# Four-layer sequence kernel on one Trainium2 core: every eighth product dt*u*B of the scans moves from VectorE to GpSimd, from a copy of B that ScalarE takes out of PSUM

## What is computed

```python
x_dbl = einsum('bsd,ed->bse', u, x_proj_w)
dt_r, B, C = split(x_dbl, [64, 80], axis=-1)
dt = softplus(einsum('bsr,dr->bsd', dt_r, dt_proj_w) + dt_proj_b)   # 512 channels
A = -exp(A_log)                                                     # 512 x 16
def step(h, (dt_t, B_t, C_t, u_t)):
    h = h * exp(dt_t[:, :, None] * A) + (dt_t * u_t)[:, :, None] * B_t[:, None, :]
    y = einsum('bdn,bn->bd', h, C_t)
```

## Time and profile before

| what | us |
| --- | --- |
| median of three runs | 2286.82 (2285.85 to 2292.27) |
| the profiled execution | 2285.53 |
| its span | 2283.7 |
| the scans in it | 89 to 1612 |
| busy: TensorE | 1945.9 (85%) |
| busy: VectorE | 1862.5 (82%) |
| busy: ScalarE | 1194.6 (52%) |
| busy: GpSimd | 1150.0 (50%) |

### The profile page before, as it was taken

One profiled execution on the slowest core, in us unless ns is written; L12 is line 12 of the kernel. 1 busy time (PEld: TensorE's weight loads), 2 busy tenths in 40 slices (PEclk: granted clock), 3 DMA queues, 4 the chain that ended last, 5 costly groups with the idle time before them and its releaser, 6 DMA issues.

```text
span 2283.7 us, 19266 instructions
## 1 busy us (share of the span) xinstructions
PE 1945.9 (85%) x6016; PEld 775.7 (34%) x6016; DVE 1862.5 (82%) x2189; ACT 1194.6 (52%) x2143; POOL 1150.0 (50%) x584
## 2 busy tenths in 40 slices
PE   6688998979899888878788888889788879999986
PEld 2223333324243233333232323234554323333323
DVE  2667989889899999889898999898766488888823
ACT  2535455445556565544555556454352246666673
POOL 2466767768878877668687777665200000000000
PEclk8799999989999999989999999999997779999998
DMA  5142122122222222222222222222014052230001
GB/s 184 39 136 61 62 65 69 53 70 68 72 65 73 72 75 70 62 65 73 63 70 70 74 71 76 68 88 83 24 61 52 8 107 30 37 43 9 2 2 37
DMA packets 80714, 143.20 MB, mean 63 GB/s; under 512 B 14587, under 2 KB 19643, under 8 KB 80076
## 3 DMA queue, kind: packets, MB, share of 16 engines
q1 hardware_dynamic: 80612, 141.98, 23.0%
HBM read 132.34 MB, written 9.01 MB: 62 GB/s over the span
## 4 chain that ended last, share of the span: by engine, by line
PE 51%; DVE 24%; POOL 11%; issue 6%; ACT 5%; DMA 1%; SPq 1%; POOLq 0%; DVEq 0%; ACTq 0%
PE psum L1562 14%; DVE hbuf L2123 12%; POOL hbuf L1312 7%; PE psum L680 5%; PE psum L1399 5%; DVE hbuf L2108 4%; PE psum L666 4%; DVE gain L956 4%; PE psum L646 4%; PE psum L561 3%; PE psum L1542 2%; PE psum L1375 2%; PE psum L1555 2%; PE psum L1423 2%; PE psum L550 2%
## 5 line engine op out<-in xcount | busy, mean ns | idle before, releaser
L1312 POOL TENSOR_TENSOR hbuf<-hbuf,cbuf 128x1024 f32<-128x1024 f32 x384 | 903.0, 2355 | 411.7 <-ACT hlast L1923 199.9
L1562 PE MATMUL psum<-hbuf,ident 128*128 128x512 f32 x1536 | 792.5, 640 | 128.2 <-POOL hbuf L1312 127.9
L1915 ACT ACTIVATE psum<-slots,cols 128x512 f32<-128x512 f32 x768 | 524.0, 686 | 461.3 <-DVE hbuf L2123 458.3
L2108 DVE TENSOR_TENSOR hbuf<-slots,psum 128x1024 f32<-128x1024 f32 x384 | 460.2, 1199 | 94.8 <-PE psum L1542 46.8
L2123 DVE TENSOR_TENSOR_SCAN hbuf<-psum,hlast,hbuf 128x512 f32<-128x512 f32 x384 | 470.3, 1265 | 17.6 <-ACT psum L1915 17.6
L2123 DVE TENSOR_TENSOR_SCAN hbuf<-psum,hbuf 128x512 f32<-128x512 f32 x384 | 447.3, 1205 | 19.0 <-ACT psum L1915 18.8
L1562 PEld LDWEIGHTS psum<-hbuf,ident 128*128 128x128 f32 x1536 | 273.3, 196 | 449.5 <-issue 270.1
L956 DVE TENSOR_REDUCE gain<-psum 128x1 f32<-128x512 f32 x512 | 314.6, 681 | 77.9 <-PE psum L646 77.7
L646 PE MATMUL psum<-slots 99*128 99x512 bf16 x512 | 212.7, 419 | 25.8 <-DVE gain L968 13.1
L511 POOL COPY wl<-hbuf 128x512 f32<-128x512 f32 x8 | 4.8, 612 | 446.8 <-PE psum L680 418.1
L1542 PE MATMUL psum<-bcs,pick 48*128 48x512 bf16 x384 | 153.1, 399 | 63.9 <-DVE hbuf L2108 61.4
(11 more groups left out here) (261 smaller groups left out, 1938.6 us busy)
## 6 DMA issues: line engine op xcount, KB each, us to landing
cbuf<-scr_c SPq DMA_DIRECT2D x384, 256.0 KB, 3.2
slots<-scr_qk SPq DMA_DIRECT2D x96, 128.0 KB
scr_qk<-slots SPq DMA_DIRECT2D x10, 512.0 KB, 2.8
wl<-in_w SPq DMA_DIRECT2D x1, 3968.0 KB, 12.2
wl<-in_ada_w SPq DMA_DIRECT2D x1, 3584.0 KB
xt<-in_x SPq DMA_DIRECT2D x2, 1024.0 KB, 12.4
wl<-in_w SPq DMA_DIRECT2D x2, 1024.0 KB, 6.9
out<-xt SPq DMA_DIRECT2D x2, 1024.0 KB, 4.7
```

The costliest lines, as they stand in the source:

```text
L1312: pool.tensor_tensor(hs, hs, cbuf[:, at % CRING:at % CRING + 1, :].to_broadcast([P, 2, TC]), ALU.mult).then_inc(weighed, 1)
L1562: last = pe.matmul(psum[:, q, :], ident[:, :], hbuf[:, at % RING, q, :], start=False, stop=n == NS - 1, skip_group_check=True)
L1915: act.activation(decay_bank(at, q), dts[k % 2][:, e, :], ACT.Exp, scale=coefficient(WORK[k], e, n)).then_inc(decay, 1)
L2108: dve.tensor_tensor(hbuf[:, at % RING, :, :], ws[k % 2][:, 2 * p:2 * p + 2, :], psum[:, 2 + at % 2:3 + at % 2, :].to_broadcast([P, 2, TC]) ...
```

## The change

Steps with at % 8 == 4, that is h = 4, 12, 20 and 28 of each chunk, 48 in all, get their product dt*u*B from GpSimd. GpSimd issues it two steps ahead, before its product with C of step at-2. ScalarE copies the broadcast B of that step from PSUM into the new buffer `bbuf` (one, of 512 columns), also two steps ahead, at the head of its step. VectorE leaves the load out. The waits on `dbu` are counted anew, over the loads that VectorE still makes; the bank of a copied B is free for the next `spread` once the copy is done.

```diff
+def by_pool(at):
+    return at % 8 == 4
+
+def loaded_by(at, pool):
+    return sum(by_pool(n) == pool for n in range(at + 1))
...
+        bbuf = sb("bbuf", [P, TC])
...
GpSimd
+            def load(at):
+                k, h = divmod(at, HALVES)
+                p = h // NS
+                pool.wait_ge(w_ready, k * KE + 2 * p + 2)
+                pool.wait_ge(b_copied, loaded_by(at, True))
+                if at >= RING:
+                    pool.wait_ge(summed, at - RING + 1)
+                pool.tensor_tensor(hbuf[:, at % RING, :, :], ws[k % 2][:, 2 * p:2 * p + 2, :],
+                                   bbuf[:, :].rearrange("p (o t) -> p o t", o=1).to_broadcast([P, 2, TC]), ALU.mult).then_inc(dbu_pool, 1)
...
                     at = j * HALVES + h
+                    if by_pool(at + 2):
+                        load(at + 2)
                     pool.wait_ge(ld_c[at % CRING], 16 * (at // CRING + 1))
...
TensorE, spread
-                if at >= 2:
-                    pe.wait_ge(dbu, at - 1)
+                if at >= 2 and by_pool(at - 2):
+                    pe.wait_ge(b_copied, loaded_by(at - 2, True))
+                elif at >= 2:
+                    pe.wait_ge(dbu, loaded_by(at - 2, False))
...
ScalarE
+            def copy_b(at):
+                act.wait_ge(bcast, at + 1)
+                n = loaded_by(at, True)
+                if n > 1:
+                    act.wait_ge(dbu_pool, n - 1)
+                act.activation(bbuf[:, :], psum[:, 2 + at % 2, :], ACT.Identity).then_inc(b_copied, 1)
...
                     at = j * HALVES + h
+                    if by_pool(at + 2):
+                        copy_b(at + 2)
                     if at not in AHEAD:
                         decays(at, 0)
...
VectorE, scan
-                dve.wait_ge(dbu, at + 1)
+                if by_pool(at):
+                    dve.wait_ge(dbu_pool, loaded_by(at, True))
+                else:
+                    dve.wait_ge(dbu, loaded_by(at, False))
...
-                    if at + 1 < TOTAL:
+                    if at + 1 < TOTAL and not by_pool(at + 1):
                         load(at + 1)
```

More of the change, by code:

```diff
@@ L349, in build @@
         diag_ready, conv_diag_ready, out_weights_ready = sem("diag_ready"), sem("conv_diag_ready"), sem("out_weights_ready")
-        bcast, dbu, decay = sem("bcast"), sem("dbu"), sem("decay")
+        bcast, dbu, dbu_pool, decay = sem("bcast"), sem("dbu"), sem("dbu_pool"), sem("decay")
+        b_copied = sem("b_copied")
         scanned, weighed, summed = sem("scanned"), sem("weighed"), sem("summed")
@@ L1180, in convolve @@
                 if k >= 2:
-                    pool.wait_ge(dbu, HALVES * (k - 1))
+                    pool.wait_ge(dbu, loaded_by(HALVES * (k - 1) - 1, False))
                 elif k == 1:
@@ L1670, in step_in @@
                 elif k >= 2:
-                    act.wait_ge(dbu, HALVES * (k - 1))
+                    act.wait_ge(dbu, loaded_by(HALVES * (k - 1) - 1, False))
                 ps, bias = take("dt", k, e), cols[:, column:column + 1]
```

## The result

The change made the kernel slower: 2306.49 us (median of 4 runs, 2304.62 to 2307.34) against 2289.55 (4 runs, 2285.85 to 2292.93) for the kernel before on the same chip, a ratio of 1.0073 with a 95% interval of 1.0053 to 1.0094, 16.9 us. The forecast was 2300 in a range of 2285 to 2315. The profiled executions have spans of 2302.9 and 2283.7 us, 19.2 apart; that of the kernel before is one of its short ones (2285.53 us, where the median is 2289.55), hence the 2 us more.

A forecast was written before the change was run, and what follows sets the result against it. The bound was taken to change hands among VectorE, TensorE and, at chunk ends, GpSimd. Terms 10.3 + 7.1 + 1.9 + 1.6 - 7.2 = +13.7 us gave 2300 us, range 2285 to 2315.

The forecast's parts named there:

- Prices: Each added GpSimd product takes 2355 ns and each added ScalarE copy 597 ns.
- Chunk ends: From step 26, GpSimd's added product delays the next chunk: 1.49 us in even chunks, 0.27 in odd, 10.3 together.
- Chunk 2: Mainly at step 18, the waiting copy and GpSimd's added product delay the product TensorE needs: 7.1 us slower.
- Chunks 3 and 4: At step 10 the decay waits behind the copy for step 12: 1.9 and 1.6 us slower.
- Gains: Saved VectorE loads that no already full TensorE follows, in chunks 5 to 11: 7.2 us faster together.
- rival C: TensorE's clock: idle times opened on a full TensorE slow its next additions, about 2320 us; chance 0.13.
- A: VectorE sets the pace throughout the scans, so 36 saved loads give 40 us: 2257 us; chance 0.10.
- B: Earlier TensorE broadcasts halve the cost of chunks 2, 3 and 4, and three more loads count: 2292 us; chance 0.20.
- D: VectorE and GpSimd stop for each other's products, up to 111 us more: 2411 us; chance 0.02.

The follow-up runs named there:

- e3: The change, but GpSimd's products go to a spare buffer and VectorE still makes all its loads; 2324.53 us, ratio 1.0147.
- e1: The kernel before with 47 of VectorE's loads left out and nothing in their place, computation incomplete; 2274.94 us, ratio 0.993.
- e5: The change without step 28, which VectorE makes again (36 products); 2297.34 us, ratio 1.0028.
- e6: The change without step 20, which VectorE makes again (36 products); 2298.72 us, ratio 1.0033.
- e11: The change without step 12 in chunks 1 to 4 (44 products); 2302.75 us, ratio 1.0057.
- e9: The change cut to eight products: step 12 in chunks 5, 6, 9, 10 and step 4 in 6, 7, 8, 10; 2289.74 us, ratio 0.9993.
- e8: The kernel before with the last dt*u of each chunk but the first made by VectorE, nothing of the change; 2294.45 us, ratio 1.0012.
- e2: The kernel before plus ScalarE's 48 copies of B, which nothing reads; VectorE keeps all its loads; 2306.13 us, ratio 1.007.
- e4: The change with ScalarE's copy moved behind both decays and the save of its step; 2306.12 us, ratio 1.0066.
- e7: The change cut to steps 4, 12 and 20 of chunks 5, 6, 7, 9 and 10 (15 products); 2287.91 us, ratio 0.9986.
- e12: The kernel before with GpSimd's last sum of dt and dt*u both moved ahead of its product of step 29; 2247.84 us, ratio 0.9836.
- e10: The kernel before with GpSimd's last dt*u before a chunk's start moved ahead of its product of step 30; 2272.13 us, ratio 0.9917.

## Why the prediction was right

The mechanism and the place of most terms held; several sizes did not, and part of the closeness is luck. Both sides of the sum came out too small: all that was added cost 33.7 us (e3), where the sum has 20.9 and, with the small costs that it books against the gains, 25.6 (an estimate from its own terms); the loads left out saved 14.4 to 16.0 (e1), where it has 7.2, or 11.9 without those costs. The two misses cancel in part.

- **Prices.** 2359 and 598 ns, as forecast. VectorE's loads stayed at 1200 ns beside GpSimd's work.
- **Chunk ends, forecast 10.3.** Measured from scan 26 to scan 31: 1.29 to 1.46 in each even chunk (forecast 1.49), between -0.02 and 0.03 in the odd ones (forecast 0.27), together 8.6. e5 took them away. The wait at `load` rose by 2.1 us behind even chunks, as forecast. That the saved load of step 28 only lengthens this wait holds for the even chunks; behind the odd ones e1 shows it worth its full 1.1 us as long as GpSimd gets no product more; in the change nothing of it is left.
- **Chunk 2, forecast 7.1.** Measured 8.35 up to scan 26. The part from scan 16 on, forecast 6.6, was 6.2, and e6 took 6.7 away; the part before it, forecast 0.5, was 2.2. Of that 1.4 stand at scan 2, behind a start at which TensorE had half clock for 10.2 us instead of 6.8; in e5, where it is 6.8 as before and the same steps are moved up to scan 26, the chunk costs 7.1. The idle time of 11 us and the side work that comes later by 7 us show it in the rows above.
- **Chunks 3 and 4, forecast 1.9 and 1.6.** The decays came 3.5 and 4.2 late (forecast 3.0 for chunk 3) and the saved load gave back 1.1. What remained up to scan 26 was 2.9 and 3.1. In chunk 4 e11 shows that the cost is not that of step 12 alone: with it gone, lateness at scans 4, 15 and 18 takes its place.
- **Gains, forecast 7.2.** Measured 2.8, chunk ends taken out. Chunks 5, 6, 9 and 10 gave 1.2, 1.4, 1.0 and 1.6 (forecast 1.4, 1.0, 1.4, 1.0). Three places failed: chunk 7 gave 0.25 of 1.1, chunk 8 cost 0.8 where 0.55 was to be gained, chunk 11 cost 1.7 where 0.8 was to be gained. This is the term that was mis-sized. In chunks 7 and 8 no full TensorE took the gain of load 12 (it had idle times of 2.3 and 0.9 us right then): scan 13 gave it back because `nmr` was held up by GpSimd's product, by 1.3 and 1.8 us. Without these 3.0 us both chunks would have gained about what was forecast, or a little more. In e1 and e9, whose `nmr` stays at 0.14 us there, scan 13 loses nothing. The sum puts this at nothing. In chunk 11 the gain goes at scans 15 to 18, in waits for decays. And of the gains that came, the 0.8 and 1.0 at scan 3 of chunks 6 and 10 are not the saved loads': chunk 6 of e8, with no load moved, has 0.9 (rival C).

So the sum was 13.7 and the scans lost 19.5; 4.4 of the difference are gains that did not come, 1.25 chunk 2, 2.5 chunks 3 and 4, less 1.7 at the chunk ends and 0.6 in chunks 0 and 1 and ahead of them. After the scans 0.3 us were gained.

**The rivals.** A (VectorE sets the pace) fell with e1. B (the handovers hide) fell: in chunks 3 and 4 they hid next to nothing, and only in 1 and 2 was the lateness at scan 10 made good, but for 0.5 us (e11). C (TensorE's clock) is half right. It gave no dozen times 1.8 us: the clock over the scans is 0.94 against 0.95. But how long TensorE stays at half clock around a chunk's start is worth up to 3 us a chunk, up and down. The traces give for four chunks the us at half clock and how much later than before scan 3 came, counted from the chunk's first scan:

| chunk | before | change | e2 | e4 | e7 | e8 | e9 |
| --- | --- | --- | --- | --- | --- | --- | --- |
| 5 | 3.4 | 3.4, -0.2 | 6.8, +1.1 | 10.2, +2.6 | 10.2, +2.9 | 3.4, 0.0 | 10.2, +3.0 |
| 6 | 6.8 | 3.4, -0.8 | 10.2, +2.4 | 10.2, +2.3 | 3.4, -0.8 | 3.4, -0.9 | 3.4, -0.9 |
| 9 | 3.4 | 3.4, -0.3 | 6.8, +1.0 | 3.4, -0.3 | 10.2, +2.8 | 10.2, +2.7 | 10.2, +3.0 |
| 10 | 6.8 | 3.4, -1.0 | 10.2, +2.3 | 3.4, -0.9 | 3.4, -0.9 | 10.2, +1.9 | 3.4, -0.9 |

The time goes with the clock, not with the edit: e8 moves no load, and e9 none ahead of scan 3 in chunks 5 and 9. (In e12, where VectorE no longer waits at the start of chunk 9, 2.8 us were lost there with 3.4 us at half clock: something else counts, which was not traced.) That blurs each of these comparisons by about 6 us in a single execution, and two chunks at the same place (5 and 9) mostly go together. D (VectorE and GpSimd block each other) fell at its size of 111 us, since the loads and scans are free of it. But it was at work in the change itself, at VectorE's small instructions: 3.0 us at `nmr` in chunks 7 and 8. e8 shows it with a larger product. The Trainium skill (SBUF — State Buffer, Who interferes with whom) limits the lock to VectorE instructions with two SBUF inputs or in a 2-port mode, and calls it exclusive. The traces agree on both sides: load and scan, with one operand in PSUM, at 1200 ns unchanged; `nmr` and e8's product, with both inputs in SBUF, held until GpSimd's product had ended (2.2 of the 2.74 us in e8).

**Open.** Why chunk 11 lost 1.7 us was not settled: in e5 it lost nothing, in e6, which keeps its step 28, 2.0, yet the loss arises at steps 12 to 18; e9, which moves no load in chunk 11, lost 1.2 there at scan 5. The 5 us after the scans are not e4's own: the traces of e9 and e10 have 4.6 and 4.9 there, and in all three 2.7 to 2.8 of it arise 50 us behind the scans, where TensorE has half clock for 6.8 us after an idle time that the kernel before passes at full clock. The rest of it was not traced. That the spread between runs (12 to 13 us in e7, e8 and e9, 10 in the 32 runs of the kernel before) comes from the clock is likely: of those 32 the nine shortest have a mean granted clock of 0.933 to 0.935, the nine longest 0.930 or 0.931. That it comes from the chunk starts above all is argued from the traces, one for each kernel.

## What to carry to other kernels

Moving work off a busy engine is worth what that engine's idle-free stretches are worth, not its busy share: measure the ceiling by leaving the work out (here 14.4 us of 52) before you pay for the copy and the second engine. Cost what is moved by its place in the in-order queue: a 0.6 us copy that waits for a result two steps ahead holds up everything behind it, here by 3.7 us, and an operation on a half-idle engine counts in full where the next stage waits for that engine's last one. And look at that last one first: the wait of 11 times 4.2 us that stood in the profile all along was worth more when a sum and a product moved up in GpSimd's queue (37 us) than the whole moved work. When GpSimd's work moves in time, look also at VectorE's small instructions with both inputs in SBUF that it may now meet.

## What the runs showed of the hardware that was not expected

- A VectorE product of 512 columns with both inputs in SBUF lasted 2741 to 2748 ns, 11 times of 11, when it met a 2.35 us product of GpSimd; it ended 0.55 us after GpSimd's. A 128x4 instruction with both inputs in SBUF, 0.13 us otherwise, lasted 1.40 and 1.89 us in the change, and ended 0.02 us after the GpSimd product that it met. Products of VectorE with one input in PSUM never showed it (1182 to 1223 ns in 384).
- After the same idle time of 4.02 us TensorE came back to full clock at different times: 3.2 us after its restart in one execution, 10.0 in another (e9), for a shift of the chunk's start by 1.1 us. Its matmuls of 512 columns take 1.06 instead of 0.59 us until then, and a kernel change of no effect there appears 3 us slower in that chunk.
